# An adaLN block with linear attention and a mixture of experts: one-time work placed between the first batches, loads on two queues, new orders on all engines

## The reference, cut to what matters

```python
x = L0_attn_x                                # (16, 512, 128)
mod = (_silu(L0_c) @ L0_wmod).reshape(L0_c.shape[0], 6, 1, -1)
sa, ca, ga, sb, cb, gb = (mod[:, 0], mod[:, 1], mod[:, 2], mod[:, 3], mod[:, 4], mod[:, 5])
ga = (2 * (ga >= 0) - 1) * jnp.maximum(jnp.abs(ga), 0.25)      # gb likewise
h = _layernorm(x, axis=-1) * (1 + ca) + sa
x = x + ga * _L0_attn_ref(h, ...)
h = _layernorm(x, axis=-1) * (1 + cb) + sb
x = x + gb * _L0_ffn_ref(h, ...)
# attention, 16 heads of 8:
q = jax.nn.softmax(q, axis=-1)
k = jax.nn.softmax(k, axis=-2)
state = jnp.einsum('bhnd,bhne->bhde', k, v)
out = jnp.einsum('bhnd,bhde->bhne', q, state)
out = (out - mu) * jax.lax.rsqrt(var + EPS) * ln_g + ln_b
return out @ Wo.T + bo
# experts: 8, each token takes the 2 with the highest probability
probs = jax.nn.softmax(x2 @ router_w, axis=-1)
top_p, top_e = jax.lax.top_k(probs, K)
# y = gelu(x @ w_in[e] + b_in[e]) @ w_out[e] + b_out[e], weighted by the probability
```

## Time and profile before

| | |
|---|---|
| median of 3 runs | 392.83 us (391.58 to 394.48) |
| the profiled execution: time | 392.8 us |
| its span (first to last instruction) | 391.1 us |
| mean granted TensorE clock | 0.965 |
| busy: PE, DVE, ACT, POOL | 362.9, 282.5, 278.5, 216.8 us |
| moved from and to memory | 42.82 MB read, 4.48 MB written |

### The profile page before, as it was taken

One profiled execution on the slowest core, in us unless ns is written; L12 is line 12 of the kernel. 1 busy time (PEld: TensorE's weight loads), 2 busy tenths in 40 slices (PEclk: granted clock), 3 DMA queues, 4 the chain that ended last, 5 costly groups with the idle time before them and its releaser, 6 DMA issues.

```text
span 391.1 us, 8091 instructions
## 1 busy us (share of the span) xinstructions
PE 362.9 (93%) x2502; PEld 327.3 (84%) x2502; DVE 282.5 (72%) x1060; ACT 278.5 (71%) x502; POOL 216.8 (55%) x221
## 2 busy tenths in 40 slices
PE   3657789999999999999999999999999999999995
PEld 3446679889999999899899999898998999988875
DVE  2665586787777888878877778788788787786432
ACT  3333679688787969696887879696969878675740
POOL 2315447373938466483838384664837383754543
PEclk9966579999999999999999999999999999999999
DMA  5570051240706071321606070605224150605061
GB/s 182 151 297 2 0 173 73 80 193 24 247 5 242 29 225 47 157 115 41 231 33 241 3 244 27 240 32 168 106 104 169 38 208 3 217 28 216 32 227 41
DMA packets 18817, 47.83 MB, mean 122 GB/s; under 512 B 2571, under 2 KB 6102, under 8 KB 18518
## 3 DMA queue, kind: packets, MB, share of 16 engines
q1 hardware_dynamic: 18576, 46.90, 33.3%
q10 hardware_dynamic: 198, 0.41, 0.3%
HBM read 42.82 MB, written 4.48 MB: 121 GB/s over the span
## 4 chain that ended last, share of the span: by engine, by line
PE 66%; DVE 9%; issue 6%; DMA 6%; POOL 5%; SPq 4%; ACT 2%; POOLq 0%; DVEq 0%; ACTq 0%
PE pY L684 19%; PE pH L672 6%; PE pH L674 6%; PE pH L673 6%; PE pB L661 4%; PE pQV L641 4%; PE pC L629 4%; PE pC L648 3%; POOL v L355 2%; DVE qn L876 2%; DMA gate_bc<-route_scratch 2%; DMA gates<-gate_scratch 2%; SPq L236 2%; DVE elg_cut L934 2%; PE pA L588 2%
## 5 line engine op out<-in xcount | busy, mean ns | idle before, releaser
L684 PE MATMUL pY<-wout,v 128*128 128x128 f32 x1024 | 128.7, 277 | 1.0 <-DVE v L958 0.7
L684 PEld LDWEIGHTS pY<-wout,v 128*128 128x128 f32 x1024 | 121.7, 193 | 2.2 <-DVE v L958 1.1
L502 ACT ACTIVATE u<-pH,cols 128x512 f32<-128x512 f32 x128 | 86.4, 689 | 49.5 <-PE pH L674 42.8
L344 POOL TENSOR_TENSOR rstd_o<-ve_o,neg_half 128x4 f32<-128x4 f32 x16 | 22.0, 1376 | 104.3 <-DVE ve_o L895 104.3
L958 DVE TENSOR_TENSOR v<-u,gate_bc 128x512 f32<-128x512 f32 x80 | 68.6, 860 | 7.0 <-DMA gate_bc<-route_scratch 3.7
L355 POOL TENSOR_TENSOR v<-u,gate_bc 128x512 f32<-128x512 f32 x48 | 63.7, 1329 | 9.0 <-DMA gate_bc<-route_scratch 9.0
L672 PE MATMUL pH<-h_hi,win_hi 128*128 128x512 f32 x128 | 54.9, 429 | 1.4 <-ACT u L502 1.4
L673 PE MATMUL pH<-h_hi,win_lo 128*128 128x512 f32 x128 | 50.6, 395 | 0.0
L674 PE MATMUL pH<-h_lo,win_hi 128*128 128x512 f32 x128 | 50.5, 394 | 0.0
L349 POOL TENSOR_TENSOR h_lo<-h,h_hi 128x512 fp32r<-128x512 f32 x16 | 22.5, 1405 | 20.2 <-ACT h_hi L440 20.2
L452 ACT ACTIVATE xn<-x_all,nmr,rstd 128x128 f32<-128x128 f32 x64 | 26.2, 482 | 4.5 <-POOL nmr L372 4.5
(11 more groups left out here) (151 smaller groups left out, 781.5 us busy)
## 6 DMA issues: line engine op xcount, KB each, us to landing
gate_bc<-route_scratch SPq DMA_DIRECT2D x64, 512.0 KB, 5.7
x_all<-in_L_attn_x SPq DMA_DIRECT2D x16, 256.0 KB, 6.9
out<-x_all SPq DMA_DIRECT2D x16, 256.0 KB, 2.0
gates<-gate_scratch SPq DMA_DIRECT2D x1, 2048.0 KB, 7.1
gb_bc<-gb_scratch SPq DMA_DIRECT2D x1, 1024.0 KB, 4.6
route_scratch<-gateT SPq DMA_DIRECT2D x64, 4.0 KB
win<-in_L_ffn_w_in SPq DMA_DIRECT2D x1, 512.0 KB, 5.6
wout<-in_L_ffn_w_out SPq DMA_DIRECT2D x1, 512.0 KB, 6.9
```

What stands on the lines that cost most here:

```text
L344: pool.tensor_tensor(rstd_o[:, :], ve_o[:, :], neg_half[:, :], ALU.pow).then_inc(s["rstdo_ready"], 1)
L502: act.activation(u[:, e % U, :], pH[:, e % 2, :], ACT.Gelu_apprx_tanh, bias=cols[:, e:e + 1]).then_inc(s["gelu_done"], 1)
L684: i = mm(pY[:, t * P:(t + 1) * P], v[:, e % U, t * P:(t + 1) * P], wout[:, e, :], start=False, stop=(e == NE - 1), skip_group_check=True)
```

## The change

Six things. (1) x loads get four semaphores of their own in turn (`x0_loaded` to `x3_loaded`); Wk and Wo are issued by ACT, Wq and Wv by SP; the 16 `b_out` loads stand ahead of the expert weights and x(2) ahead of both. (2) The broadcast of the modulation gates is split: the first two batches (256 KB) first, the other 14 later. (3) The one-time work is cut in functions (`columns`, `modulation_columns`, `attention_low`, `centring`, `gained_weight`, `attention_gates`, `expert_gates`, `expert_bias` on DVE; `turn_weights`, `modulation`, `gain_centred`, `residual_gates` on PE; `attention_weights`, `expert_high` on ACT; `expert_low` on POOL), and these stand between operations of batches 0 to 2. The waits that stood ahead of everything are now in the operation that needs them, for n == 0. `gain_centred` writes pH instead of pA. (4) Every engine has a new `step(b)`, with attention one batch further ahead than before on PE and ACT: `hT` and `kT` of b + 4 and `state` to `attend_project` of b + 3. (5) The first operations are written out one by one up to where the step loop takes over, on PE up to batch 2. (6) So are the last ones. No operation of a batch is added or left out.

```diff
...
+    FIRST = 2
+    XS = 4
...
-            sp.dma_start(x_all[:, 0, :, :], x_v[0]).then_inc(s["x_loaded"], DMA)
-            for j, wt in enumerate((Wq, Wv, Wk, Wo)):
+            def load_x(n):
+                w(sp, f"x{n % XS}_loaded", DMA * (n // XS))
+                sp.dma_start(x_all[:, n, :, :], x_v[n]).then_inc(s[f"x{n % XS}_loaded"], DMA)
+
+            load_x(0)
+            for j, wt in ((0, Wq), (1, Wv)):
...
+            def load_expert_bias():
...
+            def store_mod_gates():
                 sp.wait_ge(s["ga_ready"], 3)
                 sp.dma_start(gate_scratch, ga_rows[:, :, :].rearrange("b w c -> b (w c)")).then_inc(s["gates_stored"], DMA)
+
+            def spread_first_gates():
                 sp.wait_ge(s["gates_stored"], DMA)
-                sp.dma_start(gates[:, :, :, :].rearrange("p b w c -> p (b w c)"),
-                             gate_scratch.rearrange("(a b) n -> a (b n)", a=1).to_broadcast([P, NB * 2 * P])).then_inc(s["gates_loaded"], DMA)
-
-            def spread_moe_gates():
+                sp.dma_start(gates[:, 0:FIRST, :, :].rearrange("p b w c -> p (b w c)"),
+                             gate_scratch[0:FIRST, :].rearrange("(a b) n -> a (b n)", a=1).to_broadcast([P, FIRST * 2 * P])).then_inc(s["first_gates"], DMA)
+
+            def spread_later_gates():
...
             load_x(1)
+            load_x(2)
+            load_expert_bias()
             load_experts()
-            load_x(2)
-            spread_mod_gates()
+            store_mod_gates()
             load_x(3)
+            spread_first_gates()
+            store_moe_gates()
+            spread_later_gates()
             spread_moe_gates()
-            for b in range(-5, NB):
+            store_gates(0)
+            spread_gates(0)
+            for b in range(-1, 9):
                 step(b)
...
+            def modulation_gates(n):
+                if n == 0:
+                    pool.wait_ge(s["first_gates"], DMA)
+                if n == FIRST:
+                    pool.wait_ge(s["gates_loaded"], DMA)
...
+            masks()
+            rstd_L(0)
+            rstd_L(1)
+            h_low(0)
+            gated_weight(0)
+            h_low(1)
+            expert_low()
+            gated_const(0)
+            rstd_L(2)
+            gated_weight(1)
+            rstd_O(0)
+            rstd_B(0)
+            h_low(2)
+            gated_const(1)
...
+            for b in range(11, 21):
...
+            for j, wt in ((2, Wk), (3, Wo)):
+                act.dma_start(w_nat[:, j, :], wt).then_inc(s["w_loaded"], DMA)
+            act.dma_start(wmod_sb[:, :, :], wmod.rearrange("k (j c) -> k j c", j=NMOD)).then_inc(s["wmod_loaded"], DMA)
...
+                ln1_apply(b + 4)
+                exp_router(b + 1)
+                ek_evac(b + 3)
+                exp_q(b + 3)
+                gelu(b, 6)
+                h_evac(b + 4)
+                gateT_evac(b + 1)
+                gelu(b, 7)
+                gelu(b + 1, 0)
+                gelu(b + 1, 1)
+                qT_evac(b + 3)
+                gelu(b + 1, 2)
+                sw_evac(b + 3)
+                ln2_apply(b + 2)
+                gelu(b + 1, 3)
+                out_square(b + 3)
+                h2_evac(b + 2)
+                gelu(b + 1, 4)
+                gelu(b + 1, 5)
+                exp_k(b + 4)
...
+            attention_weights()
+            ln1_apply(0)
+            h_evac(0)
+            ln1_apply(1)
+            exp_k(0)
+            exp_q(0)
+            ek_evac(0)
+            expert_high()
+            h_evac(1)
+            qT_evac(0)
+            sw_evac(0)
+            out_square(0)
+            exp_k(1)
...
+            def gain_centred():
+                pe.wait_ge(s["gain_ready"], 1)
+                pe.wait_ge(s["cen_ready"], 1)
+                mm(pH[:, 1, 0:P], cen[:, :], gain[:, :], start=True, stop=True).then_inc(s["mm_gain"], 1)
...
+                hT(b + 4)
+                hidden(b, 7)
+                gate_turn(b + 1)
+                combine(b, 3)
+                hidden(b + 1, 0)
+                combine(b, 4)
+                hidden(b + 1, 1)
+                combine(b, 5)
+                state(b + 3)
+                q_turn(b + 3)
+                hidden(b + 1, 2)
+                state_weights(b + 3)
+                combine(b, 6)
+                combine(b, 7)
+                hidden(b + 1, 3)
+                kT(b + 4)
+                attend_centred(b + 3)
+                h2T(b + 2)
+                hidden(b + 1, 4)
+                moe_bias(b + 1)
+                hidden(b + 1, 5)
+                qv(b + 4)
+                logits(b + 2)
+                combine(b + 1, 0)
+                hidden(b + 1, 6)
+                combine(b + 1, 1)
+                ek_back(b + 4)
+                combine(b + 1, 2)
+                attend_project(b + 3)
...
+            turn_weights()
+            modulation()
...
+            for b in range(2, 12):
                 step(b)
...
+            def gained_weight():
+                dve.wait_ge(s["mm_gain"], 1)
+                dve.tensor_copy(wo_gain[:, :], pH[:, 1, 0:P]).then_inc(s["wo_gain_ready"], 1)
...
-                    attention_parts()
+                route(b + 1)
                 if has(b + 3):
                     q_shift(b + 3)
-                if has(b + 1):
-                    weigh(b + 1, 4)
+                gates_out(b + 1)
                 if has(b + 3):
                     v_bias(b + 3)
...
+            ln1_stats(0)
+            ln1_var(0)
+            columns()
+            ln1_stats(1)
+            ln1_var(1)
+            modulation_columns()
+            attention_low()
+            centring()
+            gained_weight()
+            ln1_stats(2)
+            attention_gates()
+            k_max(0)
+            q_bias(0)
+            q_max(0)
+            q_shift(0)
+            v_bias(0)
+            expert_gates()
+            q_sum(0)
+            q_inv(0)
+            q_norm(0)
+            k_inv(0)
+            state_out(0)
...
+            for b in range(4, 14):
...
```

More of the change, by code:

```diff
@@ L547, in _ @@
+            gelu(15, 7)
         @block.tensor
@@ new lines, in _ @@
+            ek_back(0)
+            hT(1)
+            state(0)
+            q_turn(0)
+            state_weights(0)
+            attend_centred(0)
+            kT(1)
+            qv(1)
+            attend_project(0)
+            ek_back(1)
+            hT(2)
+            state(1)
+            state_weights(1)
+            q_turn(1)
+            h2T(0)
+            kT(2)
+            attend_centred(1)
+            logits(0)
+            ek_back(2)
+            qv(2)
+            hidden(0, 0)
+            gate_turn(0)
@@ new lines, in _ @@
+            hT(3)
+            attend_project(1)
+            hidden(0, 1)
+            state(2)
+            kT(3)
+            state_weights(2)
+            hidden(0, 2)
+            q_turn(2)
+            hidden(0, 3)
+            hidden(0, 4)
+            attend_centred(2)
+            hidden(0, 5)
+            moe_bias(0)
+            attend_project(2)
+            h2T(1)
+            combine(0, 0)
+            qv(3)
+            logits(1)
+            hidden(0, 6)
+            hidden(0, 7)
@@ new lines, in _ @@
+            ek_back(3)
+            combine(0, 1)
+            combine(0, 2)
+            hT(4)
+            combine(0, 3)
+            state(3)
+            combine(0, 4)
+            gate_turn(1)
+            hidden(1, 0)
+            combine(0, 5)
+            q_turn(3)
+            hidden(1, 1)
+            state_weights(3)
+            hidden(1, 2)
+            combine(0, 6)
+            combine(0, 7)
+            hidden(1, 3)
+            attend_centred(3)
+            kT(4)
+            h2T(2)
@@ new lines, in _ @@
+            hidden(1, 4)
+            hidden(1, 5)
+            qv(4)
+            moe_bias(1)
+            hidden(1, 6)
+            logits(2)
+            combine(1, 0)
+            ek_back(4)
+            combine(1, 1)
+            combine(1, 2)
+            attend_project(3)
+            hidden(1, 7)
+            hT(5)
+            combine(1, 3)
+            state(4)
+            gate_turn(2)
+            hidden(2, 0)
+            combine(1, 4)
+            hidden(2, 1)
+            hidden(2, 2)
@@ new lines, in _ @@
+            combine(1, 5)
+            kT(5)
+            combine(1, 6)
+            q_turn(4)
+            hidden(2, 3)
+            state_weights(4)
+            combine(1, 7)
+            hidden(2, 4)
+            attend_centred(4)
+            h2T(3)
+            hidden(2, 5)
+            moe_bias(2)
+            qv(5)
+            logits(3)
+            hidden(2, 6)
+            combine(2, 0)
+            combine(2, 1)
+            ek_back(5)
+            combine(2, 2)
+            attend_project(4)
@@ new lines, in _ @@
+            for b in range(2, 12):
+                step(b)
+            hidden(12, 7)
+            combine(12, 3)
+            hidden(13, 0)
+            gate_turn(13)
```

(14 more changed lines are left out.)

849 lines of the change are left out of this document (616 added, 233 removed).

## The result

The changed kernel takes 413.5 us (median of 4 runs, 409.8 to 415.1) beside 393.5 for the kernel before, a ratio of 1.050 (95% interval 1.042 to 1.058). It is 5% slower; 379 us, 3.5% faster, was forecast, and 413.5 is outside the range. The profiled execution of after is the quickest of the four: 409.8 us, span 408.1.

What follows compares the result with a forecast made beforehand. PE was taken to bound the kernel between 60 and 340 us. Fill 59.0, work behind it 312.1, step waits 0.5, end waits 1.0, tail 4.5: span 377.1, plus 1.7 gives 378.8, about 379 us; range 374.5 to 387.

Steps and rivals of the forecast that it cites:

- The step: Middle of the kernel: PE work of 21.1 us per step, against 21.44 before, with nearly all waits gone.
- So each loop closes, the closest by 0.35: Middle steps: every engine delivers before PE wants it; the tightest, on ACT, takes 5.2 us and is wanted after 5.55.
- 0.5 us of waits for the 11 steps: Middle steps: PE waits 0.5 us in all, bounds 0 and 3.9 if the old wait only moves.
- The same place, slower than before: Rival, ACT's loop: 2.0 us longer than by the rows, 1.7 of wait in each of 11 steps, 398 us; 5 in 100.
- The second rival: Fill stays at low clock, or x(1) or expert weights come late: first `moe_bias` at 63, 383 us; 15 in 100.
- the first: Rival: fill as forecast, but the step keeps 21.44 us and the end its 4.4 of waits, 386 us; 18 in 100.
- The fill: Start of the kernel up to the first `moe_bias`: still at 59.0 us, bounds 56.3 to 63, with 6.4 us more done.
- The walk: Fill: the new orders timed piece by piece with durations of before, giving `hidden(0,0)` at 48.6 and `moe_bias(0)` at 59.0 us.
- 6.4 us of banked work: Fill: PE work moved ahead of the first `moe_bias`, 6.4 us, leaving 312.1 behind it.
- by 21, bounds 20 to 24.5: Fill: the first modulation gates land by 21 us, at latest 24.5, still ahead of `state_weights(0)` at 24.6.
- The clock in the fill: PE clock at full level from 31 to 34 us and again from 45; full from 31 on gives `moe_bias(0)` at 56.3.
- The end: Last batches: the wait ahead of `combine(15,0)` goes, leaving 1.0 of 4.4 us of waits, a gain of 3.4.

Runs made afterwards that it cites:

- x-early run: The changed kernel with each x load issued one step earlier on SP (load_x(b + 6) in step b), nothing else moved: 385.0 us.
- POOL held back: The changed kernel with x loads one step earlier, and POOL waiting ahead of `weigh(n, 5)` until DVE has finished `gates_out(n + 1)`: 380.9 us.

## Why the prediction was wrong, point by point

- **What failed: "The step".** "So each loop closes, the closest by 0.35" was said after placing `gate_turn`, `moe_bias`, `hT`, `rstd_B`, the broadcast gates and ACT's table load. The load of x and `ln1_stats` were not placed. The diff shows both halves: SP keeps `load_x(b + 5)`, DVE's new step does `ln1_stats` one batch further ahead. The prediction looked at SP's order in the fill and at its broadcasts in the step, but never asked when the step's x is issued and wanted. Issue 4.9 us ahead of use, landing 7.2 behind it: 2.3 us of idle DVE in a loop that runs through DVE's chain. In the sum the step that failed is the term "0.5 us of waits for the 11 steps" (bounds 0 and 3.9): the 11 steps take 262.6 for 230.7 of work, so waits and low clock are 32. Cost by the x-early run: 28.5 us.
- **No rival had it.** "The same place, slower than before" had the sign and even the rough size (1.7 per step, 398), but named a table load and a late `h_evac`. In fact it was 2.9 of wait and low clock per step, where this rival had 1.7, and it came from a DMA. ACT's stretch from `ek_evac` to `gateT_evac`, called the tightest, is on the chain of after and appears as PE's wait for `ek` (10.9 us), but with x early PE waits for `ek` in the fill alone: it follows the late x, it is not the cause. The second rival's "with both 386" does not add up if both means this one and the first: 386 and 4 are 390.
- **The step's 21.1 was right as PE's work, the wait of 0.5 was not.** With x early the 11 steps take 238.0 for 230.7 of work: 7.3 us of waits where 0.5 was taken and 3.9 was the upper bound. The step that holds two `qv` was not seen either; it takes 24.9 for 23.0 of work. The prediction took each DVE duration from before, where POOL stood elsewhere and `echosen` took 0.19; the new order of POOL put `weigh(n, 5)` and `gated_const` beside the gates. With POOL held back the steps are 21.13 and the waits 1.7. "`gate_turn` ready at 20.6, wanted at 22.2" has 1.6 of slack, which two operations stretched by 1.0 each use up.
- **The fill was right in its main term.** 56.6 against 59.0 (bounds 56.3 to 63), `hT(0)` 9.62 (9.6), `kT(1)` 27.6 (28.0), `state(1)` 34.0 (35.5), `hidden(0,0)` 44.1 (48.6). The walk ran 4.5 late at `hidden(0,0)` and 2.4 at the end. That POOL's new start, with `h_low(1)` first, pays for the 6.4 us of banked work is shown: undone, 6.1 are lost. That the gates would not delay anything "by 21, bounds 20 to 24.5" held only because of the split.
- **The clock in the fill** was 1.00 from 30 to 60 us in after, where the walk had it low from 34 to 45; hence the early end of the bounds. The rule of the Trainium skill (TensorE: Matmul & The Clock Gate, "The HAM clock gate") that the prediction cited pointed that way, though the rows that it said agree, have PE busy all through at 0.50. But with x early the clock was 0.66 from 30 to 40 and `moe_bias(0)` came at 55.8, sooner still, so the clock did not decide between 56 and 59.
- **The end was right.** From the thirteenth `moe_bias` to the end of the span it is 63.9 us in after and 74.3 in before: 10.4 less, where the forecast's 6.4 banked, 3.4 at the end and the 0.35 of two steps make 10.5 (one `h2T`, 0.4, is also done sooner than counted). `combine(15, 0)` does not wait, and putting the last turn back costs 2.4 us by the medians.
- **The sum.** With both causes removed the span is 378.4 against 377.1, the time 380.9 against 379. Part of that nearness is luck: the first `moe_bias` is 1.2 sooner than forecast (57.8) and what is behind it 2.5 longer (320.6 against 318.1).
